# Attention and a sparse feed-forward layer on one core: a third PSUM bank for the row maxima, one bank fewer for the sums of the values

## The chip, the cores and the metric

The kernel runs on one core of a Trainium2 chip. The metric is the device time of one execution in microseconds (us). The engines are TensorE (PE in the rows, its weight loads PEld), VectorE (DVE), ScalarE (ACT), GpSimd (POOL) and the queue of SyncE (SP), which issues most of the DMAs. PSUM, the memory into which TensorE writes its products, has 8 banks of 128 partitions by 512 float32.

## What is computed

```python
x = L0_attn_x                                   # (4, 512, 256)
x = _layernorm(x + attention(x, w_qkv, w_out))  # 16 heads of 16, causal mask, softmax
x = _layernorm(x + experts(x, gate, gate_up, down))
# attention
scores = jnp.einsum('bqhd,bkhd->bhqk', q, k)
scores = jnp.where(causal_mask[None, None], scores, NEG)
attn = jax.nn.softmax(scores, axis=-1)
out = jnp.einsum('bhqk,bkhd->bqhd', attn, v).reshape(b, s, HIDDEN)
# experts: the best 4 of 32 for each token, weights renormalised
gated = u * jax.nn.silu(g)
next_states = jnp.einsum('TEF,EFD->TED', gated, down_proj)
next_states = (next_states * router_weights[..., None]).sum(axis=1)
```

## The kernel before

The work is done in two parts. The first is the attention of 4 batches with the projections before and behind it, the second runs the tokens, sorted by expert, through the experts in tiles. The change touches the first part only.

The attention goes by 32 pairs of heads (8 pairs to a batch). A pair i is five slots, and in each slot one "max" unit and one "st" unit run:

- **max unit (L801 to L816, L1402 to L1414).** TensorE computes scores with the queries on the partitions and writes a full bank of PSUM (one matmul of 512 columns, or two that share the bank). VectorE adds the mask and takes the maximum along the row (`tensor_tensor_reduce`, L1412). Only the maximum (into MX) is wanted; the elementwise result has to be written somewhere, and nothing reads it. That somewhere is `sums_of`: the buffer `junk`, or part of another buffer that is not in use at the time.
- **st unit (L823 to L841, L1121).** Four pairs later (LAG = 4) TensorE computes the same scores with the keys on the partitions, from which the maxima are already subtracted because they were put into extra rows of the queries; ScalarE takes the exponential (L1125) and GpSimd zeroes what the mask hides (L1734).

The maxima reach the queries by way of "sendmax": a transpose on TensorE (L821), a split into two bfloat16 parts on VectorE (L1420, L1423) and a DMA (L593). It stands once in 10 slots, right behind the second max and st unit that follow its own pairs.

The "pv" units (L842 to L858) multiply the exponentials with the values, for a group g of two pairs: (pv, g, 0), (pv, g, 1) and (pv, g, 2) stand 2 and 3 slots apart, and all three add up in one bank. ScalarE copies that bank to RAW (L1132), and the "norm" unit transposes RAW on TensorE (L864) and divides by the sums on VectorE (L1430, L1434).

Between these stand the other units of a slot: projections to queries and keys (qk, L783, on TensorE; L1400 on VectorE), to values (v, L797), the output projection (proj, L914; L1447 to L1453 on VectorE), the logits of the router (xg, L884) and the choice of experts (fix, find, mark, place, L1465 to L1514, on VectorE). They use banks 6 and 7.

One list, `plan`, made by `make_plan`, sets the order on all engines: each engine walks it and takes its own instructions, in order. Who waits for whom is set by semaphores. The banks before are: 0 and 1 for the max units in turn, 2 and 3 for st, 4 and 5 for pv by the parity of g, 6 and 7 for the rest. The waits on TensorE that free these banks are these:

```python
kk = (rank[u] - 1) % 2                 # max: bank 0 or 1
if rank[u] > 2:
    e.wait_ge(max_free, rank[u] - 2)   # VectorE is done with the unit two before
b, r = g // 4, g % 2                   # pv: bank 4 + r
if n == 0 and g >= 2:
    e.wait_ge(raw_out, g - 1)          # ScalarE has copied group g - 2
e.wait_ge(max_free, 10 * (s + 1))      # sendmax: all maxima of its two pairs
```

TensorE works through its list in order, so while a max unit waits for `max_free` everything behind it waits as well: the st unit of the slot, the pv units and the projections.

Of the kernel before, what the change touches and what calls it, by code (L numbers as in the profile page):

```python
# [6 lines left out]
ACT = mybir.ActivationFunctionType  # L7
AX = mybir.AxisListType
F32 = mybir.dt.float32
BF16 = mybir.dt.bfloat16  # L10
I32 = mybir.dt.int32

B, S, D = 4, 512, 256
# [7 lines left out]
LAG = 4  # L21
# [13 lines left out]
PAIRS = 8 * B  # L35
QS_ROWS = ((0, 2, 3, 0), (1, 6, 1, 1), (3, 6, 1, 1), (5, 6, 1, 2))
KS_ROWS = ((0, 3, 2, 1), (1, 6, 1, 0), (2, 6, 1, 0), (5, 6, 1, 0), (4, 6, 1, 2))
QUADS = PAIRS // 2
PV_TILES = [(0,), (1,), (3, 2)]
FIRST = 6  # L40
TWO_BANKS = 8
# [170 lines left out]
def build(nc, x, xt, w_qk, w_v, w_out, gate, gup, dwn, out):  # L212
    ctx = ExitStack()
    with ctx:
# [31 lines left out]
        mneg = sb("mneg", [128, S], BF16)  # L246
        XL = sb("XL", [128, B, 4, NE], F32)
        CS = sb("CS", [128, NE], F32)
        WOT = sb("WOT", [128, 2, D], F32)
# [60 lines left out]
        AT = at("AT", [128, 2, 512], F32)  # L310
        AN = at("AN", [128, 4, D], F32)
        WO = at("WO", [128, 2, D + NE], F32)
        RAW = at("RAW", [128, 2, 512], F32)
        SM = at("SM", [128, 2, 16], F32)

        def sums_of(i, kk):

            if kk == 0:
                return junk
            return (AT if i < PAIRS // B else WOT)[:, 0, 0:256].bitcast(BF16)  # L320

        place[0] = w_end
        XG = at("XG", [128, NXG, ROW], F32)
# [15 lines left out]
        PS = ctx.enter_context(nc.psum_tensor("PS", [128, 8, 512], F32))  # L339
# [10 lines left out]
        rank = {}  # L350
# [26 lines left out]
        max_full, max_free = sem("max_full"), sem("max_free")  # L377
        nm_in = [sem(f"nm_in{r}") for r in range(2)]
        st_full, st_exp, st_mask = sem("st_full"), sem("st_exp"), sem("st_mask")
        pv_full, raw_out, sum_recip = sem("pv_full"), sem("raw_out"), sem("sum_recip")  # L380
# [259 lines left out]
        def _(e):  # L640
# [114 lines left out]
            for u in plan:  # L755
# [20 lines left out]
                elif what == "qk":  # L776
                    b, m = a
# [9 lines left out]
                elif what == "v":  # L787
                    b, half = a
# [12 lines left out]
                elif kind == "max":  # L801
                    i, n = a
# [2 lines left out]
                    elif i < LAG:  # L805
                        keep_busy(1)
                    g, r = i // 4, (i // 4) % RG
                    kk = (rank[u] - 1) % 2
                    if rank[u] > 2:
                        e.wait_ge(max_free, rank[u] - 2)  # L810
                    e.wait_ge(ld_in[r], 144 * (g // RG + 1))
                    for h, qt, c0 in pair_scores(n, 2 * (i % 4), 3, 2, 1):
                        w = 128 * (qt + 1)
# [27 lines left out]
                    t.then_inc(st_full, 1)  # L841
                elif kind == "pv":  # L842
                    g, n = a
                    b, r = g // 4, g % 2
                    if n == 0 and g >= 2:
                        e.wait_ge(raw_out, g - 1)
                    for j in PV_TILES[n]:
                        w = 512 - 128 * j
                        e.wait_ge(*free(("v", b, j // 2)))
                        for h in range(4):  # L850
                            p, o = 2 * g + h // 2, h % 2
                            piece, c0 = ((o, 0), (2 + o, 0), (4, 256 * o), (2 + o, 384))[j]
                            e.wait_ge(*((st_exp if p >= PE_MASKED else st_mask), rank["st", p, piece]))
                            t = e.matmul(PS[32 * h:32 * h + 32, 4 + r, 128 * j:512],  # L854
                                         V[b % 2][:, j, 4 * (g % 4) + h, :],
                                         PT[:, p % NPT, piece, c0:c0 + w], start=(j == 0), stop=(j == 2))
                    if n == 2:
# [144 lines left out]
        def _(e):  # L1002
# [91 lines left out]
            for u in plan:  # L1094
# [13 lines left out]
                elif kind == "part":  # L1108
                    b, m = a
                    r = (rank[u] - 1) % 2  # L1110
                    e.wait_ge(*free(("qk", b, m)))
                    e.activation(PA[:, r, 1, :], RE[:, r, :], ACT.Copy).then_inc(part1, 1)  # L1112
                elif kind == "v":
                    b, half = a
                    e.wait_ge(*full(u))
                    wait_const(e, "v1")
                    wait_pv(e, 8 * (b - 1) - 1)
                    e.activation(V[b % 2][:, 2 * half:2 * half + 2, :, 0:HD],
                                 PS[:, k, :].rearrange("p (q h d) -> p q h d", q=2, d=HD),
                                 ACT.Copy).then_inc(done, 1)  # L1120
                elif kind == "st":  # L1121
                    p, n = a
                    e.wait_ge(st_full, rank[u])
                    wait_pv(e, p - NPT)
                    e.activation(PT[:, p % NPT, n, :], PS[:, 2 + (rank[u] - 1) % 2, :], ACT.Exp).then_inc(st_exp, 1)  # L1125
                elif kind == "pv" and a[1] == 2:
                    g, _ = a
                    r = g % 2
                    e.wait_ge(pv_full, g + 1)
                    if g >= 2:  # L1130
                        e.wait_ge(*full(("norm", (g - 2) // 4, (g - 2) % 4)))
                    e.activation(RAW[:, r, :], PS[:, 4 + r, :], ACT.Copy).then_inc(raw_out, 1)  # L1132
                elif kind == "att":
                    b, c = a
                    e.wait_ge(*full(u))
                    if b:
                        e.wait_ge(*full(("proj", b - 1, 3)))
                    e.activation(AT[:, c, :], PS[:, k, :], ACT.Copy).then_inc(done, 1)
                elif kind == "dev":
                    b, = a  # L1140
                    inverse_deviation(b + 1, 4 * b, 4)
                elif kind == "lnexp":
                    b, = a
                    e.wait_ge(top_diff, b + 1)
                    e.activation(EW[:, b % 2, :, :], EW[:, b % 2, :, :], ACT.Exp).then_inc(top_exp, 1)
                elif kind == "xg":
                    b, = a
                    e.wait_ge(*full(u))
                    e.activation(XL[:, b, :, :].rearrange("p q n -> p (q n)"), PS[:, k, 0:4 * NE],
                                 ACT.Copy).then_inc(done, 1)  # L1150
                elif kind == "wot":
                    e.wait_ge(*full(u))
                    e.activation(WOT[:, :, :].rearrange("p d n -> p (d n)"), PS[:, k, :], ACT.Copy).then_inc(done, 1)
                elif kind == "rows" and a[0] != B - 2 and a[2] == 0 and (a[0] < B - 2 or a[1] == 0):
                    row_copies(a[0], a[1])
                elif u == ("open", 0):
                    wait_pv(e, PAIRS - 1)
                    rows_out_early(0)
                elif u == ("open", 1):
                    rows_out_early(1)  # L1160
                elif u == ("open", 3):
                    silu(0)
                    silu(1)
                    for j in range(4):
                        copy_down(j)
                    table_set()
# [38 lines left out]
        def _(e):  # L1205
# [181 lines left out]
            for u in plan:  # L1387
# [14 lines left out]
                elif kind == "max":  # L1402
                    i, n = a
                    s = i // 2
                    h0, kk = 2 * (i % 2), (rank[u] - 1) % 2
                    M = MX[:, s % 4, :, :]
                    e.wait_ge(max_full, rank[u])
                    if s >= 4:
                        e.wait_ge(*full(("sendmax", s - 4)))
                    for h, qt, c0 in pair_scores(n, h0, 3, 2, 1):  # L1410
                        w = 128 * (qt + 1)
                        t = e.tensor_tensor_reduce(sums_of(i, kk)[:, c0:c0 + w], PS[:, kk, c0:c0 + w], mneg[:, S - w:S],  # L1412
                                                   1.0, LOWEST, ALU.add, ALU.max, M[:, h, qt:qt + 1])
                    t.then_inc(max_free, 1)  # L1414
                elif kind == "sendmax":
# [397 lines left out]
```

## Time and profile before

| what | us |
|---|---|
| median of 3 runs | 429.66 |
| the runs | 426.7 to 431.03 |
| the profiled execution, its own time | 431.4 |
| its span, first to last instruction | 429.4 |
| TensorE busy (88% of the span) | 378.1 |
| VectorE busy (67%) | 289.5 |
| ScalarE busy (56%) | 242.5 |
| GpSimd busy (55%) | 235.9 |

The 431.4 us of the profiled execution are its span of 429.4 and 2.0 us around it. The max units begin at 22.3 us in the span and the last one leaves VectorE at 228.1. TensorE's granted clock over the whole span is 0.964 of full speed. In the rows a gap, or idle time, is what an engine waited just before an instruction, and behind the arrow stands what ended the wait.

### The profile page before, as it was taken

What the parts mean: (1) busy time and instruction counts of PE and PEld (TensorE: products, weight loads), DVE (VectorE), ACT (ScalarE), POOL (GpSimd) and SP (SyncE); (2) the same over time, 40 slices, a digit from 0 to 9 for tenths busy, and PEclk for the clock granted to TensorE, in tenths of its full rate; (3) what the DMA queues carried; (4) which work ended last, traced back from release to release, by engine and by line L of the source; (5) the groups of instructions that cost most, each with busy time, mean ns of one, the idle gap of its engine ahead of it and who ended that gap; (6) DMA issues with size and microseconds to landing.
All of it is one profiled execution on the core that took longest, in us unless ns stands there. A gap on an engine that the chain in (4) does not pass through costs nothing.

```text
span 429.4 us, 10419 instructions
## 1 busy us (share of the span) xinstructions
PE 378.1 (88%) x2826; PEld 217.2 (51%) x2826; DVE 289.5 (67%) x1159; ACT 242.5 (56%) x534; POOL 235.9 (55%) x374
## 2 busy tenths in 40 slices
PE   5979899999996799877998999997999999989880
PEld 2526554445543356433354455665676777655340
DVE  1167868885499885989789759864656666544453
ACT  2431657765545586535766628654666656546942
POOL 5321245434232585625782672777777777646872
PEclk9999999999999899968899999999999999999966
DMA  4858554755563275393727463665665656338693
GB/s 132 266 194 223 181 179 140 223 136 161 156 197 87 52 233 162 99 275 78 227 73 230 148 172 87 179 178 172 189 176 154 173 172 177 104 83 326 264 382 129
DMA packets 54071, 74.77 MB, mean 174 GB/s; under 512 B 9842, under 2 KB 45308, under 8 KB 52480
## 3 DMA queue, kind: packets, MB, share of 16 engines
q1 hardware_dynamic: 46832, 56.93, 46.6%
q0 software_dynamic: 6912, 16.93, 10.7%
q8 instruction: 25, 0.41, 0.4%
q14 instruction: 30, 0.25, 0.2%
q10 hardware_dynamic: 272, 0.26, 0.2%
HBM read 46.33 MB, written 29.66 MB: 177 GB/s over the span
## 4 chain that ended last, share of the span: by engine, by line
PE 44%; DVE 18%; SPq 16%; issue 10%; DMA 5%; ACT 3%; POOL 3%; ACTq 0%; DVEq 0%; POOLq 0%
SPq L507 13%; PE PS L854 8%; PE PS L814 6%; PE PS L783 5%; PE PS L833 5%; PE PS L797 3%; DVE WOT L1412 3%; DVE junk L1412 3%; PE PS L690 3%; SPq L489 3%; PE PS L914 2%; PE PS L712 2%; POOL scratch_slots L1753 2%; PE PS L884 2%; PE PS L739 2%
## 5 line engine op out<-in xcount | busy, mean ns | idle before, releaser
L1125 ACT ACTIVATE PT<-PS 128x512 f32<-128x512 f32 x160 | 92.0, 596 | 51.5 <-PE PS L833 47.0
L1762 POOL DMA_INDIRECT scratch_y<-Y,XG x80 | 79.8, 997 | 34.0 <-issue 18.0
L1734 POOL TENSOR_SCALAR_AFFINE_SELECT PT<-PT 128x256 f32<-128x256 f32 (+1 forms) x140 | 50.2, 367 | 77.2 <-ACT PT L1125 75.9
L1753 POOL DMA_INDIRECT scratch_slots<-XP,RI x64 | 64.0, 1000 | 40.7 <-DVE XP L1354 20.6
L814 PE MATMUL PS<-KS,QS 96*128 96x512 bf16 (+3 forms) x256 | 63.7, 310 | 19.0 <-DVE MX L1412 18.3
L1412 DVE CUSTOM_DVE_ANT_0 junk<-PS,mneg 128x512 bf16<-128x512 f32 (+3 forms) x128 | 58.4, 483 | 22.3 <-PE PS L814 22.2
L833 PE MATMUL PS<-QS,KS 98*128 98x512 bf16 (+3 forms) x256 | 63.0, 308 | 1.2 <-ACT PT L1125 0.9
L690 PE MATMUL PS<-W,XGT 128*64 x320 | 60.5, 332 | 1.1 <-DVE WG L1275 0.6
L692 PE MATMUL PS<-WG,XGT 128*64 128x192 f32 x320 | 60.6, 332 | 0.0
L1412 DVE CUSTOM_DVE_ANT_0 WOT<-PS,mneg 128x512 bf16<-128x512 f32 (+3 forms) x96 | 43.9, 484 | 9.0 <-PE PS L814 9.0
L814 PEld LDWEIGHTS PS<-KS,QS 96*128 96x128 bf16 x256 | 21.7, 100 | 55.4 <-DVE MX L1412 43.8
L1339 DVE SCALAR_TENSOR_TENSOR HH<-PS,XG,SG 128x96 f32<-128x96 f32 x80 | 24.8, 316 | 34.1 <-ACT SG L1047 31.0
L690 PEld LDWEIGHTS PS<-W,XGT 128*64 128x64 f32 x320 | 40.5, 136 | 13.1 <-issue 8.9
L854 PE MATMUL PS<-PT,V 128*32 128x256 f32 (+3 forms) x512 | 46.4, 461 | 0.0
L712 PE MATMUL PS<-W,HT 96*64 x160 | 41.6, 382 | 2.5 <-ACT HT L1054 1.4
L715 PE MATMUL PS<-WD,HT 96*64 96x256 f32 x160 | 41.6, 382 | 0.0
L692 PEld LDWEIGHTS PS<-WG,XGT 128*64 128x64 f32 x320 | 40.5, 136 | 0.0
L1063 ACT ACTIVATE Y<-PS 128x512 f32<-128x512 f32 x40 | 23.9, 598 | 25.6 <-PE PS L715 25.0
L783 PE MATMUL PS<-XT,WQ 128*128 128x512 f32 x64 | 32.8, 642 | 5.3 <-DMA WQ<-in_w_qk_dram 4.4
L1728 POOL TENSOR_TENSOR PA<-RE,PA 128x512 bf16<-128x512 f32 x16 | 18.5, 1158 | 28.7 <-ACT PA L1112 28.6
L1323 DVE COPY XGT<-PS 128x512 f32<-128x512 f32 x38 | 26.1, 688 | 9.4 <-PE PS L658 9.1
L658 PE MATMUL PS<-idf,XG 128*128 128x128 f32 x160 | 27.5, 288 | 5.0 <-DMA XG<-scratch_slots 4.2
(233 smaller groups left out, 658.1 us busy)
## 6 DMA issues: line engine op xcount, KB each, us to landing
XG<-scratch_slots SPq DMA_DIRECT2D x160, 65.0 KB, 2.6
scratch_qk<-PA SPq DMA_DIRECT2D x14, 384.0 KB, 3.1
W<-in_gate_up_dram SPq DMA_DIRECT2D x16, 288.0 KB, 3.7
KS<-scratch_qk SPq DMA_DIRECT2D x32, 128.0 KB, 3.8
YL<-scratch_y SPq DMA_DIRECT2D x8, 512.0 KB, 6.6
QS<-scratch_qk SPq DMA_DIRECT2D x8, 384.0 KB, 4.1
QS<-scratch_qk SPq DMA_DIRECT2D x24, 128.0 KB, 3.9
W<-in_down_dram SPq DMA_DIRECT2D x8, 288.0 KB, 4.8
```

What stands on the lines that cost most here:

```text
L507: e.dma_start(XG[HALF * n:HALF * n + HALF, j % NXG, :], XS[bass.ds(slot[j, n], HALF), :]).then_inc(xg_in[j % NXG], 16)
L690: e.matmul(PS[0:HALF, products_bank(j), 0:2 * FF], XGT[:, r % 2, j % 2, c, 0:HALF], W[:, bass.ds(reg[j] + 2 * FF * c, 2 * FF)], start=(c = ...
L692: t = e.matmul(PS[HALF:128, products_bank(j), 0:2 * FF], XGT[:, r % 2, j % 2, c, HALF:128], WG[:, j % 4, 2 * FF * c:2 * FF * c + 2 * FF], ...
L783: t = e.matmul(PS[:, k, :], WQ[:, c, 128 * m:128 * m + 128], XT[:, b % 2, c, :], start=(c == 0), stop=(c == 1))
L814: t = e.matmul(PS[:, kk, c0:c0 + w], QS[r][0:96, h, 128 * qt:128 * qt + 128], KS[r][0:96, h, 0:w], start=(c0 == 0), stop=True, skip_group_ ...
L833: t = e.matmul(PS[:, kk, c0:c0 + w], KS[r][0:98, h, 128 * j:128 * j + 128], QS[r][0:98, h, 128 * j:512], start=(c0 == 0), stop=True, skip_ ...
L854: t = e.matmul(PS[32 * h:32 * h + 32, 4 + r, 128 * j:512], V[b % 2][:, j, 4 * (g % 4) + h, :], PT[:, p % NPT, piece, c0:c0 + w], start=(j ...
L1125: e.activation(PT[:, p % NPT, n, :], PS[:, 2 + (rank[u] - 1) % 2, :], ACT.Exp).then_inc(st_exp, 1)
L1412: t = e.tensor_tensor_reduce(sums_of(i, kk)[:, c0:c0 + w], PS[:, kk, c0:c0 + w], mneg[:, S - w:S], 1.0, LOWEST, ALU.add, ALU.max, M[:, h, ...
L1734: e.affine_select(out=d, in_=d, compare_op=ALU.is_ge, fill=0.0, base=0, pattern=[[0, 1 if n < 2 else 2], [1, 128]], channel_multiplier=-1) ...
L1753: e.indirect_dma_start(out=XS[:, :], out_offset=bass.IndirectOffsetOnAxis(ap=RI[:, b % 2, TOPK * q + n:TOPK * q + n + 1], axis=0), in_=XP[ ...
L1762: e.indirect_dma_start(out=YK[:, :], out_offset=bass.IndirectOffsetOnAxis(ap=XG[:, j % NXG, D + 1:D + 2].bitcast(I32), axis=0), in_=Y[:, j ...
```

## The change

The max units go over three banks, 0, 1 and 5, in turn, and TensorE waits for the unit three before instead of two before. The pv units keep bank 4 alone, so that group g waits for ScalarE's copy of group g - 1. The results that nobody reads now go to three places in turn as well. `plan` is not touched: each engine has the same instructions in the same order as before, with other banks and buffers as operands and other counts in the waits; the third max unit has no wait for a bank any more, and the second group of pv has one.

```diff
+MAX_BANKS = (0, 1, 5)
...
-        def sums_of(i, kk):
-
-            if kk == 0:
+        def sums_of(i, turn):
+
+            if turn == 0:
                 return junk
-            return (AT if i < PAIRS // B else WOT)[:, 0, 0:256].bitcast(BF16)
+            if turn == 1:
+                return (AT if i < PAIRS // B else WOT)[:, 0, 0:256].bitcast(BF16)
+            if i < PAIRS // B:
+                return AT[:, 0, 256:512].bitcast(BF16)
+            if i < PAIRS - LAG:
+                return WOT[:, 1, :].bitcast(BF16)
+            return XL[:, 0:2, :, :].rearrange("p b q n -> p (b q n)").bitcast(BF16)
...
-                    kk = (rank[u] - 1) % 2
-                    if rank[u] > 2:
-                        e.wait_ge(max_free, rank[u] - 2)
+                    kk = MAX_BANKS[(rank[u] - 1) % 3]
+                    if rank[u] > 3:
+                        e.wait_ge(max_free, rank[u] - 3)
...
-                    b, r = g // 4, g % 2
-                    if n == 0 and g >= 2:
-                        e.wait_ge(raw_out, g - 1)
+                    b = g // 4
+                    if n == 0 and g:
+                        e.wait_ge(raw_out, g)
...
-                            t = e.matmul(PS[32 * h:32 * h + 32, 4 + r, 128 * j:512],
+                            t = e.matmul(PS[32 * h:32 * h + 32, 4, 128 * j:512],
...
-                    e.activation(RAW[:, r, :], PS[:, 4 + r, :], ACT.Copy).then_inc(raw_out, 1)
+                    e.activation(RAW[:, r, :], PS[:, 4, :], ACT.Copy).then_inc(raw_out, 1)
...
-                    h0, kk = 2 * (i % 2), (rank[u] - 1) % 2
+                    h0, kk = 2 * (i % 2), MAX_BANKS[(rank[u] - 1) % 3]
+                    junk_of = sums_of(i, (rank[u] - 1) % 3)
...
-                        t = e.tensor_tensor_reduce(sums_of(i, kk)[:, c0:c0 + w], PS[:, kk, c0:c0 + w], mneg[:, S - w:S],
+                        t = e.tensor_tensor_reduce(junk_of[:, c0:c0 + w], PS[:, kk, c0:c0 + w], mneg[:, S - w:S],
```

## Rows read from the trace of the kernel before

**Rows 1.** Waits from 22 to 232 us: who waited for whom, us, times, longest
```profile
DVE junk L1412 <- PE PS L814: 22.2, 19, 3.9
PE PS L814 <- DVE MX L1412: 18.3, 29, 1.8
DVE WOT L1412 <- PE PS L814: 9.0, 9, 2.1
DVE NM L1420 <- PE PS L821: 5.1, 5, 1.4
```

**Rows 2.** Busy time of each engine in stretches of the attention
```profile
core 0: us, PE busy (x) PEld busy (x) DVE busy (x) ACT busy (x) POOL busy (x), PEclk, DMA share, GB/s
...
70.00:93.00 23.00, 21.83 (x177) 10.03 (x178) 20.91 (x95) 15.92 (x30) 9.99 (x27) 1.00 0.57 169
93.00:118.00 25.00, 24.05 (x154) 13.60 (x152) 13.48 (x56) 14.38 (x28) 8.50 (x19) 1.00 0.59 166
118.00:147.00 29.00, 22.18 (x174) 11.35 (x175) 27.05 (x126) 15.34 (x28) 9.14 (x22) 0.98 0.42 116
147.00:157.00 10.00, 9.54 (x72) 4.08 (x70) 7.95 (x37) 7.17 (x12) 8.51 (x17) 0.89 0.51 151
157.00:170.00 13.00, 13.00 (x98) 8.42 (x98) 6.71 (x27) 8.56 (x15) 9.37 (x18) 1.00 0.65 200
170.00:208.00 38.00, 31.58 (x219) 14.09 (x216) 34.09 (x165) 19.49 (x35) 17.57 (x36) 0.82 0.60 166
208.00:220.00 12.00, 11.31 (x92) 5.62 (x85) 9.79 (x47) 9.19 (x17) 10.72 (x20) 1.00 0.46 144
```

**Rows 3.** Timeline of TensorE at 92 us and of VectorE at 94 us
```profile
92.37 1.88 PE L783 MATMUL PS<-XT,WQ 128*128 128x512 f32 x4
...
94.51 0.69 DVE L1412 CUSTOM_DVE_ANT_0 junk<-PS,mneg 128x512 bf16<-128x512 f32 x1 [1.23 <-PE PS L814]
```

**Rows 4.** Timeline of TensorE and VectorE at 153 us: start, duration, [idle before]
```profile
153.46 0.86 PE L854 MATMUL PS<-PT,V 128*32 128x128 f32 x16
...
154.68 0.56 DVE L1412 CUSTOM_DVE_ANT_0 WOT<-PS,mneg 128x384 bf16<-128x384 f32 x1 [0.70 <-PE PS L814]
```

**Rows 5.** Waits of VectorE from 70 to 93 us
```profile
DVE WOT L1412 <- PE PS L814: 1.2, 2, 0.6
DVE junk L1412 <- PE PS L814: 0.5, 1, 0.5
```

**Rows 6.** Waits of VectorE from 147 to 157 us
```profile
DVE NM L1420 <- PE PS L821: 1.3, 1, 1.3
DVE WOT L1412 <- PE PS L814: 0.7, 1, 0.7
```

**Rows 7.** Waits of VectorE from 170 to 220 us
```profile
DVE NM L1420 <- PE PS L821: 3.0, 3, 1.4
...
DVE junk L1412 <- PE PS L814: 0.9, 2, 0.5
...
DVE WOT L1412 <- PE PS L814: 0.6, 1, 0.6
```

**Rows 8.** Timeline around a sendmax, 187 to 191 us
```profile
187.67 0.61 PE L814 MATMUL PS<-KS,QS 96*128 96x512 bf16 x1 [1.77 <-DVE MX L1412]
...
190.50 0.38 PE L821 MATMUL PS<-idf,MX 128*16 128x128 f32 x1
...
188.38 0.69 DVE L1412 CUSTOM_DVE_ANT_0 junk<-PS,mneg 128x512 bf16<-128x512 f32 x1
...
189.00 0.69 DVE L1412 CUSTOM_DVE_ANT_0 WOT<-PS,mneg 128x512 bf16<-128x512 f32 x1
...
190.92 0.28 DVE L1420 TENSOR_SCALAR NM<-PS 16x128 bf16<-16x128 f32 x1 [1.23 <-PE PS L821]
```

**Rows 9.** Timeline of TensorE at 48 us
```profile
48.19 0.39 PE L814 MATMUL PS<-KS,QS 96*128 96x256 bf16 x2 [0.57 <-DVE MX L1412]
```

**Rows 10.** One group of pv, its copy, and the next group, 127 to 134 us
```profile
127.38 0.86 PE L854 MATMUL PS<-PT,V 128*32 128x128 f32 x16
...
128.89 0.59 ACT L1132 ACTIVATE RAW<-PS 128x512 f32<-128x512 f32 x1
...
131.59 0.60 PE L864 MATMUL PS<-idf,RAW 128*128 128x128 f32 x4
133.79 0.64 PE L854 MATMUL PS<-PT,V 128*32 128x512 f32 x4
```

## The prediction

> **What bounds the kernel now.** I read the waits first. Over the attention they show TensorE and VectorE waiting for each other at the same hand-over. TensorE stands 18.3 us before a max unit because both banks are still with VectorE, and VectorE stands 22.2 and 9.0 us before a maximum because no scores are there [rows 1]. Two engines that both wait at one hand-over are short of buffers wherever these waits alternate. Where only one of them waits, the other is simply the slower one, and a buffer gives nothing. So I next cut the attention into stretches and asked of each which engine is the slow one [rows 2]. Three kinds come out:
>
> - TensorE alone is slow. From 157 to 170 us it is busy 13.00 of 13.00 us and VectorE 6.71; from 93 to 118 it is busy 24.05 of 25. Here the projections stand between the max units: four matmuls of a qk unit take 1.88 us, and VectorE waits 1.23 us for the next scores [rows 3]. TensorE doesn't wait for a bank here, so a third bank is of no use inside such a stretch. Most of the 31 us that VectorE waits for scores lies here.
> - VectorE alone is slow. From 118 to 147 us it is busy 27.05 of 29 us, from 170 to 208 it is busy 34.09 of 38. This is where it also does the residual sums, the choice of experts and the places. TensorE waits, and nearly all of its 18.3 us are here. They can't be won back, because VectorE has no more to give than its own idle time.
> - Both wait in turn: 70 to 93, 147 to 157 and 208 to 220 us. TensorE waits for a bank, then a pv unit of 0.86 us stands between two max units, and VectorE runs dry for 0.70 us [rows 4]. Here a third bank helps: TensorE may be one unit further ahead when the pv unit begins.
>
> **The change part by part.** What a third bank can win is therefore what VectorE idles in the last two kinds of stretch, not what TensorE waits. I add it up from the waits of VectorE.
>
> From 70 to 93 us these are 1.2 + 0.5 = 1.7 us [rows 5]. TensorE itself is idle only 23 - 21.83 = 1.2 us there [rows 2], so the gain lies between 1.2 and 1.7; I take 1.4.
>
> From 147 to 157 us they are 1.3 + 0.7 = 2.0 us [rows 6], against 10 - 9.54 = 0.5 us that TensorE is idle [rows 2]. I take the middle, 1.3. The 1.3 us of it before L1420 are of the kind that the next term explains.
>
> From 170 to 220 us they are 3.0 + 0.9 + 0.6 = 4.5 us [rows 7]. The 3.0 before L1420 come from sendmax, and the place at 187 us shows how. TensorE waits 1.77 us for a bank, and only then come the max unit, its st unit, a pv unit and, last, the transpose of sendmax at 190.50. VectorE is through with its two maxima after 189.00 and stands idle 1.23 us until 190.92 [rows 8]. With a third bank that max unit waits for the unit before, and all that follows, the transpose included, begins up to 1.77 us earlier, which is more than the 1.23 us that VectorE lacks. I count two of the three in full (2.6 us, since their longest is 1.4 and the one shown is 1.23) and take the other 1.9 us of the stretch against TensorE's idle 12 - 11.31 = 0.7 us [rows 2], the middle of which is 1.3. That makes 3.9.
>
> The other part is the lead itself. Each time a stretch in which VectorE sets the pace ends and TensorE becomes the slow one, TensorE is now one max unit further on, and keeps that to the end. One unit of VectorE is the distance of two maxima, 189.00 - 188.38 = 0.62 us [rows 8], some 0.65 with the two-piece units. There are four such changes: near 36 us, near 48 us, where TensorE waits 0.57 us just before the qk units begin [rows 9], near 93 us [rows 3] and near 157 us [rows 2]. That is 4 x 0.65 = 2.6 us. There is no fifth at the end, since the last sendmax waits for the last maximum anyway.
>
> Next to these the costs are small. sendmax waits for all maxima of its two pairs. Before, this wait was always met, as the max unit before it in the queue had already waited for the same count. Now it can be the one that ends last. Behind it stand the next max unit and all else on TensorE, but that max unit needs the same count itself under three banks, so the wait only moves from one instruction to its neighbour; I cost it at 0, with 0.3 us for each of 16, 4.8 us, as the upper bound if the transpose then runs too late for VectorE. That end would take 9.2 to 4.4 and stays inside the range.
>
> The pv units have one bank now, and (pv, g, 0) waits for ScalarE's copy of the group before. In the rows the last pv of a group ends at 128.24, the copy at 128.89 + 0.59 = 129.48, and the next group begins at 133.79: 4.3 us of room. What is more, the transposes at 131.59 on the same queue have already waited for the same copy [rows 10]. I cost it at 0. If that cover were gone, the price would be 129.48 - 128.24 = 1.24 us for each of 15 groups, 18.6 us.
>
> The places of the unread results cost nothing: the same number of bytes is written on the same partitions. No row shows a change of buffer with a price, and `junk` and WOT take turns before with waits that differ by what precedes them alone. I put it at 0 with 0.01 us for each of 256 instructions on either side, an estimate from the 0.69 us that a maximum takes into either place [rows 8], so 2.6 us at worst.
>
> The sum is 1.4 + 1.3 + 3.9 + 2.6 = 9.2 us. Its lower end is 1.2 + 0.5 + 2.6 + 0.7 = 5.0 with no leads, its upper end 1.7 + 2.0 + 4.5 + 2.6 = 10.8. The part behind the attention has no edit, and its start hangs on VectorE's last work of the attention, so I let the gain reach the end in full. From the profiled execution's own 431.4 us this makes 422.2. That execution lies above the three runs shown (426.7 to 431.03, median 429.66), so the forecast for the median is 429.66 - 9.2 = 420.5 us. About 1%, 4.3 us, is what a measurement of this kernel can tell from no change.
>
> TensorE's granted clock is 0.82 of full speed from 170 to 208 us, 0.89 from 147 to 157 and 0.98 from 118 to 147 [rows 2]. As there are only two levels, 1.2 and 2.4 GHz, this is 38 x 0.36 + 10 x 0.22 + 29 x 0.04 = 17 us at the lower one, and each such stretch follows waits of TensorE such as the 1.77 us [rows 8]. I leave the clock where it is: the stretches in which VectorE sets the pace stay, and TensorE's waits in them with them.
>
> [...]
>
> **The rivals.**
>
> *The wait only moves.* TensorE gets its third bank and is then held by something else at the same distance: sendmax, or banks 6 and 7 of the other units, which VectorE frees in the same order. Then only the four leads are won, 2.6 us, and the time is 427.1, within 1%. For it speaks that sendmax now binds once in 10 slots; against it that the max unit with its 18.3 us is the only large wait of TensorE for VectorE in the list [rows 1].
>
> *The single bank of the values.* This ends slower. If ScalarE came to the copy late, the first pv unit of each group would hold TensorE for it. At 1.24 us for each of 15 groups less the 9.2 won this is 9.4 us more, 439.1; it decides from 9.2 / 15 = 0.6 us a group on. Against it stand the 4.3 us of room and the transposes in between [rows 10]. I hold it for very unlikely.
>
> *The clock.* Also slower. TensorE's remaining waits fall elsewhere, and the stretches at 1.2 GHz move from where VectorE sets the pace to where TensorE does, 93 to 118 or 157 to 170 us. A stretch of 7 us of TensorE's work at half speed costs 3.5 us. Three of them would eat the gain, and four give 429.66 - 9.2 + 14 = 434.5. For it speaks that 17 us at the lower level exist today; against it that the granted clock is 1.00 in both of these stretches, where TensorE doesn't rest [rows 2].
>
> **How the numbers follow.** I give the forecast (a gain of 5 us or more) 78%, "the wait only moves" 16%, the clock 4% and the single bank 2%. The likeliest time is 420.5. The range reaches up to the first rival, 427.1, and a little over it, 428; down it goes to 429.66 - 10.8 = 418.9, less the 3 us by which a run of this kernel lies below the median, less a bit for clock won back, so 415. Faster by over 1% is 0.78, within 1% 0.17, slower 0.05.
>
> **What would show it.** In the changed kernel's profile TensorE's waits at the max unit should fall from 18.3 to some 10 us, part of it now before the transpose of sendmax; VectorE's waits before the split of the maxima (L1420) should be under 1 us instead of 5.1; the 31 us of VectorE before its maxima should fall by 3 to 5 only, as those behind projections stay. The last maximum should leave VectorE near 219 us instead of 228. ScalarE's copy of the values should hold nobody. I am wrong if the last maximum comes at 225 us or later, if VectorE still waits before the split of the maxima, or if the time behind the attention grows by what was won in it.

## The result, and the profile after

The changed kernel takes 425.23 us (median of 20 runs, 421.52 to 430.74), the kernel before 429.74 us (20 runs, 426.7 to 434.89) on the same chip. The ratio is 0.989, 95% interval 0.987 to 0.992. That is 4.5 us, 1.1%, in the direction of the forecast, inside its range, and about half of the 9.2 us that its sum gave. Ratios and intervals leave out runs that lie over 1.5% above the fastest of the same kernel, so a ratio here and below need not be that of the two medians.

First the waits of the changed kernel from 22 to 232 us, which answer to [rows 1]. From here on "after" is the changed kernel; its line numbers are 7 higher for TensorE and ScalarE and 8 higher for VectorE from the maxima on, so L1420, L1428, L821, L828 are the maxima, the split of the maxima, the max unit and the transpose of sendmax.

```profile
DVE junk L1420 <- PE PS L821: 15.4, 12, 4.2
PE PS L821 <- DVE MX L1420: 8.5, 15, 1.2
DVE WOT L1420 <- PE PS L821: 7.9, 6, 2.1
DVE AT L1420 <- PE PS L821: 7.2, 9, 1.8
PE PS L828 <- DVE MX L1420: 4.9, 5, 1.7
PE PS L840 <- ACT PT L1132: 2.1, 5, 0.6
DVE NM L1428 <- PE PS L828: 1.6, 3, 0.7
```

TensorE's wait for a bank has fallen from 18.3 to 8.5 us. Another 4.9 us now stand before the transpose of sendmax, as the prediction said; 1.7 of them, at the last sendmax, were there before. VectorE's waits before the split of the maxima fell from 5.1 to 1.6. TensorE waits nowhere for the RAW copy: the single bank of the values holds nobody.

The same stretches as in [rows 2], in the changed kernel:

```profile
core 0: us, PE busy (x) PEld busy (x) DVE busy (x) ACT busy (x) POOL busy (x), PEclk, DMA share, GB/s
70.00:93.00 23.00, 22.30 (x179) 10.18 (x178) 21.25 (x99) 16.36 (x30) 10.73 (x28) 1.00 0.62 177
93.00:118.00 25.00, 23.55 (x154) 13.40 (x152) 13.91 (x55) 14.23 (x28) 8.42 (x18) 1.00 0.58 173
...
147.00:157.00 10.00, 9.77 (x77) 5.08 (x75) 8.95 (x42) 7.76 (x13) 8.76 (x16) 1.00 0.64 201
...
170.00:208.00 38.00, 31.10 (x246) 14.22 (x244) 36.72 (x178) 23.27 (x41) 20.37 (x43) 0.96 0.68 178
208.00:220.00 12.00, 11.97 (x88) 7.00 (x87) 10.15 (x46) 7.49 (x13) 10.62 (x20) 1.00 0.32 108
```

From 170 to 208 us VectorE is busy 36.72 us instead of 34.09, so it seems to have won 2.6 us there, just the term of the prediction. The granted clock in the same row has gone from 0.82 to 0.96 as well. That one pair of profiles can't tell which of the two did it, and this turned out to be the point on which the forecast missed.

The last maximum leaves VectorE at 221.5 us; these are its last two results in the changed kernel:

```profile
221.06 0.08 DVE L1420 DVE_READ_ACCUMULATOR2_ANT MX<- 128x1 f32 x1
221.40 0.08 DVE L1420 DVE_READ_ACCUMULATOR2_ANT MX<- 128x1 f32 x1
```

It was 228.1 before. Counted from the start of the first maximum (22.7 and 23.9 us) the attention takes 197.5 us instead of 205.4, so 7.9 us less, but the span only went from 429.4 to 426.1, by 3.3. The pair loses 1.2 us ahead of the first maximum (TensorE's clock rose to the full level at 10.6 us in that execution, at 9.2 in the one of before) and about 1.6 us right behind the last. That second loss is seen on TensorE behind the last maximum:

```profile
221.63 0.27 PE L828 MATMUL PS<-idf,MX 128*16 128x128 f32 x1 [1.66 <-DVE MX L1420]
221.76 0.38 PE L840 MATMUL PS<-QS,KS 98*128 98x512 bf16 x1
221.97 0.22 PE L846 MATMUL PS<-idb,mneg 128*128 128x128 bf16 x1
222.12 1.86 PE L861 MATMUL PS<-PT,V 128*32 128x512 f32 x8
223.92 0.61 PE L840 MATMUL PS<-QS,KS 98*128 98x384 bf16 x2
```

After a wait of 1.66 us the pv unit's eight matmuls take 1.86 us; at the full clock such eight take 1.07. The rest of the 3.3 against 7.9 lies in the part behind, which differs by 2 to 3 us between executions of one kernel (below).

### The profile page after: what moved, and what is told of

The parts are those of the page before. It is cut to its first block, busy times and chain, and to the rows that moved or that the text cites. A ratio compares the mean times of both kernels' runs of the same rounds, so it can differ in the third digit from the quotient of the medians.

```text
span 426.1 us, 10418 instructions
## 1 busy us (share of the span) xinstructions
PE 375.2 (88%) x2826; PEld 215.9 (51%) x2826; DVE 289.4 (68%) x1159; ACT 242.5 (57%) x534; POOL 235.4 (55%) x374
## 4 chain that ended last, share of the span: by engine, by line
PE 55%; DVE 17%; issue 9%; DMA 7%; ACT 3%; SPq 3%; POOL 3%; ACTq 0%; DVEq 0%; POOLq 0%
PE PS L697 9%; PE PS L861 7%; PE PS L719 6%; PE PS L840 5%; PE PS L790 5%; PE PS L821 5%; PE PS L665 4%; PE PS L804 3%; DVE WOT L1420 3%; PE PS L921 3%; DVE junk L1420 2%; DMA YL<-scratch_y 2%; SPq L514 2%; POOL scratch_slots L1761 2%; DMA scratch_y<-Y,XG 2%
## 5 line engine op out<-in xcount | busy, mean ns | idle before, releaser
L821 PE MATMUL PS<-KS,QS 96*128 96x512 bf16 (+3 forms) x256 | 61.9, 303 | 9.6 <-DVE MX L1420 8.5
L840 PE MATMUL PS<-QS,KS 98*128 98x512 bf16 (+3 forms) x256 | 62.1, 305 | 2.8 <-ACT PT L1132 2.5
L1420 DVE CUSTOM_DVE_ANT_0 WOT<-PS,mneg 128x384 bf16<-128x384 f32 (+3 forms) x117 | 52.0, 481 | 8.2 <-PE PS L821 7.9
L1420 DVE CUSTOM_DVE_ANT_0 junk<-PS,mneg 128x512 bf16<-128x512 f32 (+3 forms) x86 | 39.4, 485 | 15.4 <-PE PS L821 15.4
L1346 DVE SCALAR_TENSOR_TENSOR HH<-PS,XG,SG 128x96 f32<-128x96 f32 x80 | 24.9, 316 | 33.7 <-ACT SG L1054 30.5
L821 PEld LDWEIGHTS PS<-KS,QS 96*128 96x128 bf16 x256 | 21.7, 99 | 41.8 <-DVE MX L1420 25.9
L1070 ACT ACTIVATE Y<-PS 128x512 f32<-128x512 f32 x40 | 23.9, 599 | 25.7 <-PE PS L722 23.8
L790 PE MATMUL PS<-XT,WQ 128*128 128x512 f32 x64 | 33.4, 653 | 5.8 <-DMA WQ<-in_w_qk_dram 4.6
L1736 POOL TENSOR_TENSOR PA<-RE,PA 128x512 bf16<-128x512 f32 x16 | 18.5, 1156 | 29.3 <-ACT PA L1119 29.2
L1282 DVE COPY WG<-W 128x384 f32 x80 | 27.7, 388 | 6.9 <-issue 6.9
```

The source lines that it names most:

```text
L790: t = e.matmul(PS[:, k, :], WQ[:, c, 128 * m:128 * m + 128], XT[:, b % 2, c, :], start=(c == 0), stop=(c == 1))
L821: t = e.matmul(PS[:, kk, c0:c0 + w], QS[r][0:96, h, 128 * qt:128 * qt + 128], KS[r][0:96, h, 0:w], start=(c0 == 0), stop=True, skip_group_ ...
L840: t = e.matmul(PS[:, kk, c0:c0 + w], KS[r][0:98, h, 128 * j:128 * j + 128], QS[r][0:98, h, 128 * j:512], start=(c0 == 0), stop=True, skip_ ...
L1420: t = e.tensor_tensor_reduce(junk_of[:, c0:c0 + w], PS[:, kk, c0:c0 + w], mneg[:, S - w:S], 1.0, LOWEST, ALU.add, ALU.max, M[:, h, qt:qt + 1])
```

## The experiments

Four theories were tried; D came up with the second group of runs. A: the gain is the lead of the max units alone, and the 2.6 us of VectorE from 170 to 208 us in the profile of before were no property of the kernel. B, the mechanism of that: they came with the stretches in which TensorE's granted clock was at 1.2 GHz, the lower of its two levels. C: the missing half was lost in the drain behind the last maximum. D: it was lost at a place near 87 us where the scores of the second kind (st) wait. The rival of A is the prediction itself, with other parts of the change costing something.

Two of the four groups of runs landed on chips where every version's median is 484 to 496 us. The attention lasts as long there (205.1 us in a second profile of before, whose execution took 492.45 us), only the part behind it is 50 to 60 us longer. There the medians tell less, and I read the attention's own length from the profiles.

**The change without its lead.** TensorE may be two units ahead, as before; the three banks, three places and the one bank of the values stay.

```diff
-                    if rank[u] > 3:
-                        e.wait_ge(max_free, rank[u] - 3)
+                    if rank[u] > 2:
+                        e.wait_ge(max_free, rank[u] - 2)
```

> The changed kernel with its three banks for the maxima, its one bank for the values and its three places for the unread results, but TensorE waits for the unit two before, as in the kernel before. It tells the cost of the other parts of the change from the gain of the lead. If these parts are free, as the prediction says, it is within 0.5% of before and the last maximum comes 205 us after the first. If the single bank of the values or the third place costs what is missing from the forecast, it is 3 to 5 us slower than before (1.0%), and the missing time shows between the first and the last maximum.

Measured: 491.43 us beside 492.36 of before, ratio 0.991 (0.978 to 1.003): not told apart. Once more, on another chip:

> The changed kernel with only the lead taken back: the maxima rotate over three banks and three places, the sums of the values keep one bank, but TensorE may again fill a bank only when VectorE is at most two units behind (the wait is for rank - 2). Theory A (the whole gain is the lead, the other parts are free): the time is that of the kernel before, 429.8, within 1.3 us, and the last maximum ends near 225 us of the span, as in a profile of before without low-clock stretches. Rival (the single bank of the values or the third place costs or gives something by itself): it leaves before's time by more than 2 us on either side; slower means that the single bank costs, faster that the change gains without its lead.

Measured: 487.04 beside 487.41, ratio 0.9991, interval 0.9963 to 1.002. The last maximum ends at 227.9 (226.0 in the first). Within 0.4%, 1.9 us, the other parts of the change cost and give nothing. The gain of 4.5 us is that of the lead.

**More executions of both kernels.** The changed kernel beside the second group's before, and before's profile again.

> The changed kernel, unchanged, profiled once more and timed. Theory A: the last maximum comes 197 to 199 us after the first one (197.6 in the first profile), 7 to 8 us less than before, and the time is about 4.5 us less than before, so 2 to 3 us are lost behind the last maximum. If the stretch at the lower clock near 220 us is what loses them, it is there again or the time behind the last maximum is 1.5 us shorter than the first profile's 204.6. Rival B: the distance is 200 us or more, and nothing is lost behind it.

> The changed kernel, unchanged, profiled a third time and timed. From the first to the last maximum: 197 to 200 us (197.5 and 199.3 so far), so 6 to 8 us less than before. Theory A (what is won reaches the end but for what a low clock takes while the attention drains): the time is 5 to 7 us less than before. Rival B (2 or 3 us of it are always given back behind the last maximum): the time is 4 to 5 us less, and the time from the last maximum to the end is 2 to 3 us longer than before's on the same chip.

> The kernel before, unchanged, profiled a third time. From the first to the last maximum it took 205.4 and 205.1 us in the two profiles so far; 204 to 207 us is expected again, whatever chip it is and however long the rest takes.

Measured: 485.47 beside 492.36 us on the slower chip, ratio 0.978 (0.965 to 0.991, from two runs of the changed kernel); 424.39 beside 429.79 on the other, ratio 0.988 (0.983 to 0.992). The attention took 199.3 us in after_again, which had 6.8 us at 1.2 GHz between 24 and 31 us; after and after_b had none there. In before_b it took 202.0 us where 204 to 207 were expected, so its length differs by over 3 us between executions. This further profile of before is the telling one. Its row for 170 to 208 us, and TensorE from 187 us on, which answers to [rows 8]:

```profile
170.00:208.00 38.00, 29.70 (x245) 13.96 (x244) 36.51 (x177) 21.75 (x39) 19.41 (x39) 1.00 0.65 171
```

```profile
187.77 0.39 PE L814 MATMUL PS<-KS,QS 96*128 96x512 bf16 x1 [1.77 <-DVE MX L1412]
188.00 0.38 PE L833 MATMUL PS<-QS,KS 98*128 98x512 bf16 x1
188.31 1.07 PE L854 MATMUL PS<-PT,V 128*32 128x512 f32 x8
189.30 0.28 PE L821 MATMUL PS<-idf,MX 128*16 128x128 f32 x1
...
189.10 0.69 DVE L1412 CUSTOM_DVE_ANT_0 WOT<-PS,mneg 128x512 bf16<-128x512 f32 x1
...
189.71 0.27 DVE L1420 TENSOR_SCALAR NM<-PS 16x128 bf16<-16x128 f32 x1
```

It is the same program, with the same 1.77 us wait of TensorE for a bank. But its pv unit takes 1.07 us and not 1.94, the transpose comes at 189.30 and not at 190.50, and VectorE goes from the maximum to the split without a gap. With the clock at 1.00, two banks already keep VectorE busy 36.51 of 38 us, as much as three do. Nothing was left for the third bank to win here.

**Theory D: SyncE's order.** In the changed kernel SyncE sent the maxima of group 4 at 82.95 us though they were ready at 80.74, and an st unit stood 0.55 us at 87.35. Here they are sent ahead of two x loads, by moving the last two loads of x four steps and the spare rows two steps later in the plan.

```diff
-        put((18, 36, 52, 54)[b], ("x", b))
+        put((18, 36, 56, 58)[b], ("x", b))
-        put(40 + 3 * n, ("lead", n))
+        put(42 + 3 * n, ("lead", n))
```

> The changed kernel with the fills of the spare rows and two loads of x some slots later in the plan, so that on SyncE's queue the maxima of pair group 4 go out before them. In the changed kernel they are ready at 80.7 us and issued at 82.95, and the st unit that needs them waits 0.55 us at 87.35. Theory D (the queue of SyncE has become the limit there, which takes the lead that should be kept near 93 us): the issue comes 1.2 to 1.4 us earlier, the wait at that st unit is gone, and the last maximum comes 0.4 to 1 us earlier, counted from the first; the time is up to 1 us less. Rival: the st unit waits for ScalarE there, and nothing changes (within 0.2 us at that place).

Measured: 423.9 beside 429.79 us, ratio 0.988 (0.983 to 0.993), the same as the change alone. The wait is gone. From max unit 40 to 66 this execution takes 21.4 us, where after_b and after take 21.9 and 22.0; but after_again, with the old order, takes 21.4 as well. So at that place the order was worth 0.5 us at most, and D falls as an explanation of 4.7 us. The attention lasts 196.4 us here, 1.5 less than in after_b, but 1.4 of that lie between units 80 and 117, where after_b has 3.4 us at 1.2 GHz and this execution none. Without such a stretch there, after takes the same 46.5 us for these units, and fill_end (below) 47.2.

**Theory C: the drain.** Seven unread matmuls (`keep_busy`, 512 columns each, here with the bank as a second argument) go into a free bank while TensorE waits for the last maxima.

```diff
+                    if s == QUADS - 1:
+                        e.wait_ge(max_free, 5 * PAIRS - 2)
+                        keep_busy(7, MAX_BANKS[(5 * PAIRS - 3) % 3])
```

> The changed kernel with 7 small matmuls into a free bank in TensorE's wait of 1.7 us before the last transpose of the maxima, so that TensorE is not idle just before it drains the attention. Theory C (the lower clock at the end of the attention gives back 1.5 us): the stretch at 1.2 GHz near 220 us is gone, the values' matmuls of 512 columns (eight of them) there take 1.06 us instead of 1.86, and the time is 1 to 2 us less than the changed kernel's. Rival: the clock falls there anyway or fell only in that one execution, and the time is within 0.2% of the changed kernel's.

> The kernel with 7 small matmuls in TensorE's wait before the last transpose of the maxima, profiled and timed once more. Theory C (a low clock while the attention drains gives back 1.5 us): 1 to 2 us less than the changed kernel in this same call. Rival: within 0.7 us of it.

Measured: 490.36 beside 492.36 us, unclear; then 425.69 beside 429.79, ratio 0.992, against 424.39 for the change alone. The attention lasts 197.5 us as in after. The low clock is not at the drain in this execution but at 246 us; nor is it at the drain in after_b, which has no filling. C falls: this filling doesn't give the missing time back, and what the drain loses in one execution it doesn't lose in another.

**Theory B, by filling TensorE's waits.** The kernel without the lead, which at the full clock should show no waits before the split. First a coarse version, filling ahead of every max unit from pair 16 on:

```diff
+                    if i >= 16:
+                        e.wait_ge(max_free, rank[u] - 3)
+                        keep_busy(2 if i >= 24 else 1, kk)
+                    if rank[u] > 2:
+                        e.wait_ge(max_free, rank[u] - 2)
```

> As the kernel without the lead, but from pair 16 on TensorE puts one (from pair 24 on two) small unread matmuls of 512 columns into the free third bank before it waits for rank - 2. It does not change what the third bank gives; it takes away the short idle times of TensorE before the maxima. Theory B (the 2.6 us of VectorE's waits in 170 to 208 us of the profile of before came with the stretches at 1.2 GHz, not from the shortage of banks): no low clock behind 147 us, VectorE busy over 36 us of the 38 from 170 to 208, the end of the last maximum 225 us or earlier, and the time 1 to 2 us under that of the kernel without the lead. Rival (they came from the banks): VectorE's waits of 2 us and more for the transpose of the maxima stay although the clock is full, last maximum 227 or later, and the fills make it 1 to 3 us slower.

Measured: 496.48 beside 487.41 us, the last maximum at 235.3. TensorE is now busy 17.00 of 17 us from 208 to 225: the fill made it the bound. The time says nothing on B. The second version fills only ten waits that are there anyway, with less than each lasts:

```diff
+                    fill = {90: 4, 94: 5, 97: 2, 100: 5, 126: 3,
+                            130: 2, 132: 6, 136: 4, 139: 4, 142: 6}
+                    if rank[u] in fill:
+                        e.wait_ge(max_free, rank[u] - 3)
+                        keep_busy(fill[rank[u]], kk)
+                    if rank[u] > 2:
+                        e.wait_ge(max_free, rank[u] - 2)
```

> The kernel without the lead (wait for rank - 2), and ten of TensorE's waits before maxima between 131 and 203 us (those of 0.75 to 1.8 us in the trace of before) are filled with 2 to 6 unread matmuls of 512 columns each into the free third bank, chosen to be shorter than the wait. Theory B (VectorE's waits for the transposes between 170 and 208 came with the clock at 1.2 GHz): the granted clock stays at 1.00 from 147 to 208, VectorE is busy over 36 of the 38 us, its waits for the transposes there are under 0.7 us in sum, the last maximum is at or before 225, and the time is 0 to 2 us under before's. Rival (they belong to the shortage of banks): over 2 us of such waits stay, last maximum about 228.

> The kernel before, once more, for a further profile. Theory B: VectorE's waits for the transposes of the maxima between 170 and 208 us go up and down with the low-clock time of the same stretch: 2.6 us with 13.7 us at 1.2 GHz, none with none. Rival: they are about 2.6 us here as well, whatever the clock.

The stretches of the version with the fills, then its waits of VectorE from 170 to 208 us (its lines are 4 higher again, so L1424 is the maxima):

```profile
147.00:170.00 23.00, 22.58 (x176) 13.14 (x174) 15.63 (x71) 16.54 (x28) 19.04 (x35) 1.00 0.59 180
170.00:208.00 38.00, 35.09 (x270) 16.22 (x270) 36.16 (x177) 21.67 (x39) 19.78 (x40) 1.00 0.66 171
208.00:225.00 17.00, 14.82 (x107) 8.58 (x106) 14.86 (x69) 11.39 (x21) 14.90 (x28) 1.00 0.44 136
```

```profile
DVE junk L1424 <- PE PS L825: 0.6, 1, 0.6
```

The clock is 1.00, the waits before the split are gone, VectorE is busy 36.16 us and the last maximum ends at 224.6, all without a third bank's lead. Still the whole takes 431.15 us beside 429.28, ratio 1.0045 (1.0026 to 1.0063), where 0 to 2 us less were expected. The part behind the last maximum takes 206.2 us here and 201.3 to 203.7 in three profiles of before; why was not tried. This execution also lost 1.6 us before its first fill, between 24 and 31 us at 1.2 GHz (unit 26 ends 28.9 us after the first maximum's start, 27.3 in before_b). So the clock explains VectorE's waits, but the fills brought nothing to the end.

The third execution of before (431.09 us) has the clock at 0.96 from 170 to 208 and no wait before the split either. All executions profiled, in that stretch:

| lead there | granted clock | VectorE's wait before the split, us | VectorE from max unit 117 to 144, us | executions |
|---|---|---|---|---|
| no | 0.82 | 2.6 | 40.3 | before, first profile |
| no | 0.87 | 1.7 | 39.7 | lead_early_b |
| no | 0.91 | 1.9, 1.8 | 39.4, 39.3 | no_lead, lead_early |
| no | 0.96 | 0 | 37.7 | before_c, before again on the slower chip, no_lead_b |
| no | 1.00 | 0 | 37.6 | before_b, fills_in_waits |
| yes | 0.91 | 0 | 37.9 | lead_late_b |
| yes | 0.96 to 1.00 | 0 | 37.7 to 37.9 | after, after_again, after_b, fill_end, fill_end_b, nm_first, lead_late |

(Units count the 160 fillings of a bank; the coarse filling is left out, as TensorE is its bound.) Without the lead the waits come at 0.91 and below and never above. There are eight of them, and in each the transpose lies inside a stretch at 1.2 GHz. With the lead none came at 0.91 either, in the one execution that had it.

The row of lead_late_b, with the clock low and VectorE busy all the same:

```profile
170.00:208.00 38.00, 32.84 (x248) 15.72 (x247) 36.75 (x177) 22.18 (x40) 18.99 (x39) 0.91 0.63 170
```

That looks as if the third bank lets the transpose come early enough for VectorE, as the prediction's term has it. It isn't shown. In none of the eight executions with the lead does a stretch at 1.2 GHz lie over a transpose of sendmax there; in lead_late_b the clock is low from 195.3 to 202.1 us and the transposes are at 175.3, 188.1 and 202.9. The place that tests it is the sendmax near 150 us. Without the lead VectorE waits 0.9 to 1.3 us before that split in the five executions with a stretch at 1.2 GHz just ahead of the transpose, and not at all in the four without one. With the lead it waits 0.65 to 0.87 us in the four with such a stretch, and not at all in the four without. (The coarse filling is left out again.) One of these four, lead_late:

```profile
147.23 1.94 PE L861 MATMUL PS<-PT,V 128*32 128x512 f32 x8
149.09 0.38 PE L828 MATMUL PS<-idf,MX 128*16 128x128 f32 x1
...
149.51 0.28 DVE L1428 TENSOR_SCALAR NM<-PS 16x128 bf16<-16x128 f32 x1 [0.87 <-PE PS L828]
```

So at the low clock the third bank shortens such a wait and doesn't remove it, and at the full clock there is none to remove.

**Half of the lead.** Only up to pair 15, and only from pair 16:

```diff
-                        e.wait_ge(max_free, rank[u] - 3)
+                        e.wait_ge(max_free, rank[u] - (3 if i >= 16 else 2))
```

> The lead is given for the units of pairs 0 to 15 only, later units wait for rank - 2. Theory A puts 2.8 us of the 4.1 us that the attention gains before pair 16 (the end of unit 80): time 427.0, the last maximum 2.5 to 3 us earlier than without the lead. Theory of the prediction (the gain lies mostly behind, in the stretch of 170 to 220 us and the leads of 93 and 157 us; 4.7 of 9.2 us before): 425.1 or less here. Rival (the early gain is only lent, taken back behind at the loads and the exponentials): 429 to 430.

> The lead is given for the units of pairs 16 to 31 and the remaining ones only. Theory A: 1.3 us is gained in the attention behind unit 80, so 428.5, and the two halves add up to the whole change's 4.5 us. The prediction's sum would put 3.9 + 1.3 and a lead of 0.65, so 5.9 us, in this half: 423.9. If both halves alone give about 4 us, a lead anywhere is enough and they don't add up.

> The lead for the units of pairs 0 to 15 only. Its profile on the other chip had unit 80 1.8 to 2 us earlier than without the lead, and the last maximum at 224.3. Theory A: 2 to 2.8 us faster than before (427.0 to 427.8 at 429.8). Rival (an early lead is only lent): within 1 us of before.

> The lead for the units from pair 16 on only. Theory A: 1.3 to 2 us faster than before (428 at 429.8), the two halves together 4 to 4.5 us. The prediction's sum had 5.9 us in this half (423.9).

(The diff is that of the late half; the early one has `i < 16`.) On the slower chip: early 485.57 beside 487.41 us, ratio 0.9995 (0.996 to 1.003); late 483.89, ratio 0.979 (0.972 to 0.985), which rests on two runs of eight at 474.8 and 479.8, while the other six took 483.6 to 484.8; I make nothing of it. On the other: early 428.20 beside 429.28, ratio 0.9965 (0.9931 to 0.9998), so 1.5 us; late 427.80, ratio 0.9984 (0.9956 to 1.0012), so 0.7 and not told from nothing. Together 2.2 us (2.6 by the medians), where A expected 4 to 4.5 and the whole change gives 4.5 to 5.2. Halves are worth less than half. In the early half's profile the stretch from 170 to 208 has the clock at 0.87 and the old waits of 1.7 us; the late half's has 6.8 us at 1.2 GHz near 144 us. The attention lasts 201.4 to 202.5 us in the four profiles of the halves, 202.0 to 205.4 in the four of before and 196.4 to 199.3 in the six with the whole lead. The intervals are as wide as the shortfall, so whether it is real stays open.

## Why the prediction was right and wrong

The step that failed is the term of 3.9 us for 170 to 220 us, within it "I count two of the three in full (2.6 us ...)", together with "I leave the clock where it is". The 2.6 us are no fixed price of two banks. They are what this kernel pays in an execution with 6.8 us or more at 1.2 GHz in that stretch (38 x 0.18, from a granted clock of 0.91). Of eight profiled executions without the lead there and without fills, four had such waits, 8.0 us in sum, so 1.0 us each on the average. The profiled execution was the one with the lowest clock of the eight. The row with 0.82 had been read, and priced only as something that might get worse. What the third bank would save of such a wait is not shown for this stretch; near 150 us it saved 0.4 us or so of 0.9 to 1.3. The 1.3 us of [rows 6] before the split, counted in the term for 147 to 157 us, is that wait near 150 us and hung on the clock in the same way.

The attention of before_b, an execution with the clock at 1.00 there, against that of after_b tells the terms one by one. These are the ends of the same max units on VectorE, each from the start of the first maximum:

| up to max unit (us in before_b) | before_b | after_b | won in the stretch | forecast |
|---|---|---|---|---|
| 26 (50) | 27.3 | 26.7 | 0.6 | 0.65, lead near 36 |
| 40 (70) | 47.4 | 46.0 | 0.8 | 0.65, lead near 48 |
| 66 (93) | 70.4 | 67.8 | 1.1 | 1.4 |
| 80 (119) | 96.4 | 93.6 | 0.2 | 0.65, lead near 93 |
| 117 (168) | 145.2 | 141.6 | 0.9 | 1.3 + 0.65, lead near 157 |
| 144 (206) | 182.9 | 179.5 | -0.3 | 2.6 |
| last (225) | 202.0 | 197.9 | 0.7 | 1.3 |
| sum | | | 4.1 | 9.2 |

- The first three terms came within 0.3 us: a third bank does win VectorE's waits where both engines wait in turn, and a lead of about one unit (0.6 and 0.8 us) is kept where TensorE becomes the slow one.
- The leads near 93 and 157 us brought less. TensorE's waits for ScalarE before st went from 0.4 us, once, to 2.0, five times, so a part of the lead may run into the exponentials. That is only argued: none of the five stands between units 66 and 80, so what takes the lead near 93 us stays open; one, of 0.4 us, stands at 150.5 us. The forecast of 1.95 us for units 80 to 117 also held the wait near 150 us that comes with the clock. Both executions have a stretch at 1.2 GHz near 144 us, and before_b another at 132.
- From 208 us on 0.7 was won instead of 1.3. The middle of the two bounds (0.7 and 1.9) was taken where the lower was right.
- The wait of sendmax cost nothing that shows, as said; neither did the single bank of the values nor the places (ratio 0.9991 without the lead). The rival "single bank" and the clock as a loss fell: the granted clock stayed at 1.00 from 93 to 118 and from 157 to 170 us.
- The Trainium skill, "TensorE: Matmul & The Clock Gate", section "HAM oscillation — how this bites in real kernels", tells of a kernel whose loop was reordered so that TensorE stays at its full clock, and in which double-buffering in PSUM gave no further gain. Here a third bank gave 1.1%, with 1.1 us where both engines wait in turn, from 70 to 93 us; in the stretch from 170 to 208 us, at the full clock, it gave nothing.
- "Reaches the end in full" holds only on the average. The last maximum ends at 228.1, 225.0, 226.5 in three executions of before, mean 226.5, and at 221.5 and 221.7 after: 5.0 us earlier, against 4.5 us of median time. It was forecast at 219 from the one profile's 228. By single profiles the part behind it takes 201.3 to 203.7 before and 201.7 to 204.6 after.

The second error lies in how the sum was anchored. The sum was taken from an execution of 431.4 us, above the three runs shown, and then set on the median in full. What makes one execution longer than the median can't be won from the median. The waits that hang on the low clock are not all of it: before_b had none of them from 170 to 208 us and took 430.7 us all the same, with 2.4 us more behind its last maximum than the first profile.

Of the tells, TensorE's bank waits (8.5 for "some 10"), the wait moved to sendmax, and the copy that holds nobody were right. VectorE's waits before its maxima are 30.5 us in sum over the three places; the 31.2 of [rows 1] left out a line for AT, which in before_b is 2.3 us beside 21.9 and 9.0, 33.2 in sum. So they fell by about 3, the lower end of the 3 to 5 forecast. The split's waits are 1.6 us in one profile and 2.1 in the other where under 1 was forecast, and the prediction had named such waits as a sign of being wrong. Two profiles of before have 2.3 and 1.6 as well, so the fall from 5.1 is not the change's.

## What to carry to other kernels

Before pricing a wait of one profile, read the granted clock in the same stretch, and look at a second execution. A wait behind matmuls at 1.2 GHz, such as 1.94 us for a pv unit that takes 1.07, belongs to that execution and enters the sum only as often as it occurs. A third buffer gains nothing in a stretch where the consumer is already busy 36.5 of 38 us; it gained about one unit at two of the places where the consumer stops being the slow one, and less at the others.

## What the runs showed of the hardware that was not expected

- The same program at the same point had the clock at 0.82, 0.96 and 1.00 from 170 to 208 us in three executions, with the same wait of 1.77 us ahead. Stretches at the lower level came near the same places (132, 145, 185 to 204 us), but not in each execution: between 22 and 232 us they make 17.1 us in before and none in nm_first.
- Filling waits did not take the low clock out of the execution. With the last wait filled it sums to 25.0 us over the whole execution, against 18.5 and 22.8 in after and after_b. With ten waits filled, 31 to 225 us were at 1.00, and the sum is 26.7 us against 26.0 to 33.4 in three executions of before; the whole was 0.45% slower. With one profile of each filling on such a chip, how much of this is chance stays open.
- The chip matters more than the change. Before takes 429.3 to 429.8 us on some and 487.4 to 492.4 on others, at the same length of the attention. In the profile of the longer ones ScalarE has waits in the experts' part whose end the profile puts down to "remote" and to none of the core's own instructions. The waits of before from 290 to 420 us on such a chip (the second profile of before):

```profile
POOL scratch_y L1762 <- ACT Y L1063: 43.0, 24, 3.3
...
ACT SG L1047 <- remote: 13.3, 4, 6.1
...
ACT Y L1063 <- remote: 11.8, 3, 4.8
```

Such "remote" waits are not among the largest of the same stretch on a chip of the first kind. What they are was not looked into.
